# First stage of a vision layer: GpSimd subtracts the low parts of Q's weights from pieces that ScalarE scales in place, and K's and V's low parts are made four tokens later

## What is computed

```python
# token stage: one S4 convolution kernel per batch row b (64), token h (128), 1024 positions l
dt = exp(log_dt); dt_Lambda = dt * Lambda          # complex, 128 tokens x 64 states
Wc = W * (exp(dt_Lambda) - 1) / (exp(dt_Lambda * 1024) - 1) / Lambda
K  = real(einsum('chn,hnl->chl', Wc, exp(dt_Lambda * pos)))      # W is the input x; h = K, (64, 128, 1024)
# layer stage, per batch row of 128 tokens
h = h + attention(layernorm(h), Wq, Wk, Wv, Wo)    # 32 heads of 32, 8 kv heads, rotary, causal
h = h + ffn(layernorm(h), A, B, Wr, br)            # 8 low-rank experts, softmax router
```

## Time and profile before

| | before |
|---|---|
| median of 3 runs | 2348.03 us (2345.55 to 2348.85) |
| profiled execution, its own time | 2350.26 us |
| its span | 2348.1 us |
| TensorE busy / VectorE / ScalarE / GpSimd over the span | 95% / 77% / 75% / 75% |
| VectorE busy in each stretch of 10 us from 40 to 230 us | 8.9 to 10.0 us |
| last matmul of the first stage ends | 239.3 us |
| first instruction of the second block | 244.6 us |

### The profile page before, as it was taken

The page is one execution under the profiler, slowest core; times in us unless marked ns, Lnnn a source line. Parts: engine busy times, 40 slices in busy tenths (PEclk is TensorE's granted clock), DMA queues, the critical chain, the costliest instruction groups (busy, mean ns, idle before and its releaser), DMA issues.

```text
span 2348.1 us, 49641 instructions
## 1 busy us (share of the span) xinstructions
PE 2231.6 (95%) x14040; PEld 1147.6 (49%) x14040; DVE 1818.7 (77%) x7750; ACT 1760.8 (75%) x6141; POOL 1750.0 (75%) x1550
## 2 busy tenths in 40 slices
PE   3898699999999999999999999999999999999986
PEld 2777344444444444444444444444444444444442
DVE  8999467777777777777777777877777777777864
ACT  5787477777787777777777777777778777778772
POOL 3776387777777778777778778788777777778772
PEclk9999899999999999999999999999999999999988
DMA  3888599999999999999999999999999999999994
GB/s 95 268 268 259 126 176 181 193 188 186 194 194 186 189 196 181 195 193 186 192 194 188 187 191 192 188 195 191 186 197 190 189 192 192 181 196 192 190 166 105
DMA packets 1205661, 443.10 MB, mean 189 GB/s; under 512 B 1155718, under 2 KB 1158022, under 8 KB 1205388
## 3 DMA queue, kind: packets, MB, share of 16 engines
q1 hardware_dynamic: 1205380, 439.93, 95.9%
q10 hardware_dynamic: 8, 0.01, 0.0%
HBM read 87.43 MB, written 67.11 MB: 66 GB/s over the span
## 4 chain that ended last, share of the span: by engine, by line
PE 67%; DMA 6%; POOL 6%; DVE 4%; SPq 3%; issue 2%; ACT 2%; POOLq 0%; DVEq 0%; ACTq 0%
PE pc L910 11%; PE pb L910 10%; PE pa L910 10%; DMA pt<-p 4%; PE pb L896 4%; PE pb L898 4%; PE pb L897 4%; PE pa L896 4%; PE pa L897 4%; PE pa L898 4%; PE pv_ps L939 3%; PE s_ps L924 3%; POOL p L1436 3%; POOL pr L1428 2%; DMA h_ln<-h 2%
## 5 line engine op out<-in xcount | busy, mean ns | idle before, releaser
L1063 ACT ACTIVATE pr<-pr,smin 128x64 f32<-128x64 f32 (+1 forms) x2048 | 738.8, 362 | 185.3 <-DVE smin L1207 184.4
L1428 POOL TENSOR_TENSOR pr<-pr,rinv 128x512 f32<-128x512 f32 x512 | 577.0, 1137 | 367.8 <-DVE rinv L1215 366.8
L1436 POOL TENSOR_TENSOR p<-pr,p 128x512 f16<-128x512 f32 x512 | 590.9, 1158 | 66.6 <-ACT p L1073 64.6
L1207 DVE CUSTOM_DVE_ANT_0 pr<-s_ps,cst 128x64 f32<-128x64 f32 (+1 forms) x2048 | 404.2, 252 | 219.0 <-PE s_ps L924 119.0
L1073 ACT ACTIVATE p<-pr 128x512 f16<-128x512 f32 x512 | 320.1, 625 | 257.8 <-DMA pt<-p 133.6
L1063 ACT ACTIVATION_READ_ACCUMULATOR pr<-pr,smin 128x1 f32 x2048 | 382.3, 187 | 0.0
L910 PE MATMUL pa<-wkv_hi,xt 128*128 128x512 f16 x1024 | 326.5, 380 | 13.4 <-DMA xt<-xs 13.4
L910 PE MATMUL pb<-wq_hi,xt 128*128 128x512 f16 x1024 | 326.9, 381 | 0.0
L910 PE MATMUL pc<-wq_hi,xt 128*128 128x512 f16 x1024 | 315.2, 379 | 0.0
L635 PE MATMUL hps<-z,xw 128*128 128x256 f32 x792 | 178.8, 386 | 60.5 <-POOL xw L363 38.2
L896 PE MATMUL pa<-wo_hi,ctx_t 128*128 128x512 f16 x512 | 195.5, 382 | 2.0 <-DVE ctx_t L1221 1.8
(11 more groups left out here) (185 smaller groups left out, 4723.5 us busy)
## 6 DMA issues: line engine op xcount, KB each, us to landing
h<-rows SPq DMA_DIRECT2D x128, 256.0 KB, 4.0
h_res<-h SPq DMA_DIRECT2D x64, 512.0 KB, 4.6
out<-rows SPq DMA_DIRECT2D x64, 512.0 KB, 3.4
h_ln<-h SPq DMA_DIRECT2D x63, 512.0 KB, 4.5
pt<-p SPq DMA_TRANSPOSE x512, 4.1
xa<-x SPq DMA_DIRECT2D x16, 256.0 KB, 4.4
xb<-x SPq DMA_DIRECT2D x32, 128.0 KB, 3.8
wst<-wq SPq DMA_DIRECT2D x8, 512.0 KB, 4.9
```

The costliest lines, as they stand in the source:

```text
L1063: last = A.activation(p, p, ACT.Exp, bias=smin[g % 2][:, j:j + 1], scale=-1.0, accum_out=rsum[g % 2][:, j:j + 1])
L1207: V.tensor_tensor_reduce(pr[g % 2][:, cols], s_ps[g % 2][:, cols], masks[h], 1.0, 3e38, ALU.add, ALU.min, smin[g % 2][:, j:j + 1]).then_in ...
L1428: nc.gpsimd.tensor_tensor(p3, p3, rinv[g % 2][:, :].unsqueeze(2).broadcast_to([P, HG, P]), ALU.mult).then_inc(p_norm, 1)
L1436: nc.gpsimd.tensor_tensor(p[:, HG * P:], pr[g % 2][:, :], p[:, 0:HG * P], ALU.subtract).then_inc(pl_done, 1)
```

## The change

- Q's low parts are no longer made by VectorE. ScalarE, right behind each Q piece's high part, multiplies the piece in its buffer by 64 in place (one more instruction for each of 8 pieces), and GpSimd subtracts the high part from it, at the end of window 3 of the chunk (behind `add`).
- K's and V's low part stays on VectorE and moves from the end of window 0 to the end of window 1 of the next chunk. O's stays at the end of window 3, those of `aw` and `bm` at the ends of windows 5 and 9. In the last chunk O's and K's and V's come at the very end, as before.
- SyncE waits for GpSimd's count where the buffer held a Q piece, for VectorE's elsewhere, and its waits and loads move with the low parts: from the third chunk on, Q's next piece from window 1 to window 2 of the chunk, ahead of O's, and K's and V's from window 3 to window 0 of the next.

```diff
-LOW_LATER = 1
+        def low_at(piece):
+            at, name, k, _, _ = piece
+            return WINDOWS if k == CHUNKS - 1 and name != "wq" else at + (2 if name in ("wq", "wkv") else 1)
+
+        def pieces_before(n, on_pool):
+            return sum((name == "wq") == on_pool for _, name, _, _, _ in PIECES[:n])
...
-                    if n >= WR:
-                        sp.wait_ge(w_lo, n - WR + 1)
+                    if n >= WR and PIECES[n - WR][1] == "wq":
+                        sp.wait_ge(wq_low, pieces_before(n - WR + 1, True))
+                    elif n >= WR:
+                        sp.wait_ge(w_lo, pieces_before(n - WR + 1, False))
...
-                    while loaded < len(PIECES) and PIECES[loaded - WR][0] + LOW_LATER <= w + 1:
+                    while loaded < len(PIECES) and low_at(PIECES[loaded - WR]) <= w + 1:
                         load_weight(loaded)
...
+                def wq_lo(n):
+                    _, name, k, width, _ = PIECES[n]
+                    pool.wait_ge(wq_scaled, k + 1)
+                    nc.gpsimd.tensor_tensor(weight("wq_lo", k), wst[n % WR][:, 0:width], weight("wq_hi", k),
+                                            ALU.subtract).then_inc(wq_low, 1)
...
                     add(w)
+                    for n, piece in enumerate(PIECES):
+                        if piece[1] == "wq" and low_at(piece) == w:
+                            wq_lo(n)
...
-                    A.activation(weight(name + "_hi", k), wst[n % WR][:, 0:width], ACT.Copy, scale=WS).then_inc(w_hi, 1)
+                    staged = wst[n % WR][:, 0:width]
+                    A.activation(weight(name + "_hi", k), staged, ACT.Copy, scale=WS).then_inc(w_hi, 1)
+                    if name == "wq":
+                        A.activation(staged, staged, ACT.Copy, scale=WS).then_inc(wq_scaled, 1)
...
                     for n, piece in enumerate(PIECES):
-                        if piece[0] + LOW_LATER == w:
+                        if low_at(piece) == w and piece[1] != "wq":
                             weight_lo(n)
-                weight_lo(len(PIECES) - 1)
+                for n, piece in enumerate(PIECES):
+                    if low_at(piece) == WINDOWS and piece[1] != "wq":
+                        weight_lo(n)
```

More of the change, by code:

```diff
@@ L219, in s4_stage @@
         w_lo = sem("w_lo")
+        wq_scaled = sem("wq_scaled")
+        wq_low = sem("wq_low")
         tab_v = sem("tab_v")
```

## The result

The changed kernel takes 2362.28 us (median of 5 runs, 2360.26 to 2363.53) against 2348.03 us: 1.0056 times the time before, 95% interval 1.0044 to 1.0067 (the bare quotient of the two medians is 1.0061). The profiled execution took 2363.53 us, its span is 2361.7. In a second measurement, on another chip, the same kernel took 2360.35 against 2350.14 us there, 1.0044 times (1.0027 to 1.0060). The forecast was 2358.5 us and slower.

A forecast was written before the change was run, and what follows sets the result against it. VectorE was taken to set the pace (busy 24.81 of 24.91 us), a closed loop after the change. Terms +2.6, -0.8, +1.1, +6.4 and +1.2 gave +10.5 us: median 2348.0 to 2358.5, likeliest range 2354 to 2364, wide 2340 to 2366.

The forecast's parts named there:

- up to the first `wo_lo`: Start to VectorE's first `wo_lo`: later `table_i` and GpSimd's chain give 63.2 us against 60.61, +2.6.
- first cycle: First stretch from one VectorE `wo_lo` to the next: 26.4 us against 27.19, as `aw_lo`'s wait falls away, -0.8.
- the four others: Last four of six cycles, `wo_lo` to `wo_lo`: 26.3 to 26.9 us against 24.9, together +6.4.
- end of the stage: Window 30: `sum_z` meets the last `add`, then the subtraction, +2.3 us, less the removed `wq_lo`, 1.13: +1.2.
- VectorE and GpSimd take turns: Their instructions with two SBUF inputs never run together; `wkv_lo` loses its 2.2 us wait, `tables` waits, `digits` follows the `add`.
- The subtraction: GpSimd, behind window 3's `add`: 1024 columns, 2.25 us, bounds 2.1 and 2.6, added to the chain.
- ScalarE's 0.95 us: Scaling pass over 1024 columns behind `wq_hi`, ahead of the sines: `theta` comes 0.95 us later.
- The closed loop: TensorE's windows 3 and 0, ScalarE, GpSimd's chain, `tables`: `table_i` at 14.3 plus chain 12.0, cycle at least 26.3 us.
- SyncE's moved loads I cost at nothing: First-stage load queue: stores behind moved loads late by under 1 us; otherwise up to +1.3 a cycle, +8 in all.
- Rival 1: First stage: the subtraction does not keep VectorE from its turns; cycles 23.3 us, -14, total 2334; chance 0.11.
- Rival 2: `digits` gets its turn between `digits_m2` and the `add`, 2.36 off the chain; cycles 24.0 us, -7, 2341; chance 0.12.
- Rival 3: Half the waits, `theta` about 1 us earlier than said; cycles 25.2 us, total 2348 to 2352; chance 0.15.

The follow-up runs named there:

- e11: Changed kernel with GpSimd's subtraction over 64 of the 1024 columns of each Q piece: 2353.60 us, 1.0021 times the kernel before.
- e3: Changed kernel without ScalarE's scaling, so GpSimd subtracts from the unscaled Q piece: 2353.61 us, 1.0031 times the kernel before.
- e7: Changed kernel with SyncE's load into the buffer of O's piece issued one window later: 2359.45 us, 1.0041 times the kernel before.
- e10: Changed kernel with GpSimd's `add` for window 0 held back until VectorE's `digits` are done: 2364.66 us, 1.0062 times the kernel before.
- e4: Changed kernel with ScalarE's three sines moved to the end of window 0, ahead of Q's high part: 2348.91 us, 1.0014 times the kernel before.
- e6: Kernel before with ScalarE's three sines moved to the end of window 0, ahead of Q's high part: 2352.02 us, 1.0009 times the kernel before.
- e2: Changed kernel with K's and V's low parts back at the end of window 0; Q's stays on GpSimd: 2362.50 us, 1.0063 times the kernel before.
- e1: Kernel before with only K's and V's low parts made four tokens later; Q's stays on VectorE: 2344.17 us, 0.9989 times the kernel before.

## Why the prediction was right, point by point

**Direction and size.** Slower, with the reason named. The first stage was forecast 10.5 us longer and is 8.5 to 8.9; the other 5.1 us of the first measured difference (14.25 us) lie in the second block, of which the prediction said nothing. Without these 5.1 us the median would have been near 2357, below the forecast and not above it (an estimate, 2348.0 + 8.9). In the second pair of profiles the marks are 10.5 apart. Term by term, from the first pair:

| term | forecast | measured |
|---|---|---|
| up to the first `wo_lo` | +2.6 | +1.8 |
| first cycle | -0.8 | -0.2 |
| second cycle | +1.1 | +0.4 |
| the four others | +6.4 | +6.1 |
| end of the stage | +1.2 | +0.8 |

**VectorE and GpSimd take turns: right.** It carries all the rest. `wkv_lo` at 0.68 us, `tables` at 2.84 and L504 behind the `add`, at 2.57, are as foretold. But the 2.84 of `tables` came by another order, so that this number is in part luck: I had `tables` wait for the subtraction in all cycles. That is so in the first two (2.61 us, from 81.81 on, the chain from `table_i` to `wo_lo` 11.67). In the others `table_i` ended after `sum_z` was issued, `sum_z` went ahead of the `add`, and `tables` waited for the `add` (185.13 to 187.93) and ran ahead of the subtraction. The chain is then 11.43 instead of 12.0. In the first two cycles L504 is issued late in the `add` and lasts only 0.82 us. The reading of `digits` in the sum of VectorE's own work was off, too: they hold it for 0.87 us (162.76 to 163.63 in the earlier trace rows), not 0.67; the chain does not use that figure.

**The subtraction: right, and a little cheaper than taken.** It took 2.13 us where it ran unhindered (55.44); 2.25 was taken, with bounds of 2.1 and 2.6. e11 shows its worth: 7.8 us of the first stage.

**ScalarE's 0.95 us: right.** The start-to-start is 0.94, and e3 takes 0.7 to 0.9 us off each of the last three cycles.

**The closed loop: right in kind, wrong in one link.** I closed it through TensorE's 12.3 us of windows 3 and 0 without a gap, so that window 0 is done at 10.5, with TensorE idle for some 3 us ahead of window 3. The third cycle has such a gap (2.20 us, from 111.58 to 113.78). In the fifth TensorE's timeline is another:

```profile
159.77 12.67 PE L659 MATMUL hps<-z,xw 128*128 128x256 f32 x56 [1.99 <-ACT rows L433]
173.37 10.60 PE L659 MATMUL hps<-z,xw 128*128 128x256 f32 x48 [0.94 <-issue]
```

The first row is windows 2 and 3, the second windows 0 and 1. TensorE waits for ScalarE's evicts ahead of window 2, and starts window 0 at 173.37, 4.2 us after `wo_lo`, right behind VectorE's first `table_z` for it; with 5.42 us for its 24 matmuls it is done at 9.6. What holds `theta` back there is a store (3.02 and 0.61 us above): `wq_hi` starts at 11.45 and `table_i` at 14.7, 0.4 later than the 14.3 taken. In the second, fourth and sixth cycle these two starts are the same within 0.1 us. In the second ScalarE waits 0.92 us for a store; in the fourth and sixth the profile puts the 3.13 and 2.01 us ahead of the same evict down to TensorE, but in e7, with the load out of the way, that evict runs at 6.2 instead of 8.0 to 8.2.

The term that was too small is thus "SyncE's moved loads I cost at nothing", with its buffers late "by under 1 us": one was 3 us late. The fallback beside it was up to 1.3 us a cycle, and e7 shows 1.3 us of `theta` and 1.1 of a cycle for that queue. The store behind O's load is issued 1.6 us after `wo_lo` in both kernels (140.34 before, 170.81 after). Before the change the evict of window 0's first token ran 5.5 us behind it (145.82) and waited last for TensorE; now it runs 6.2 us behind it (177.04) and waits for the store. The store lands at least 0.7 us later, and TensorE's earlier window 0 no longer covers it. New just ahead of that store is the moved load of Q's piece (167.13). That this load delays it is read from the rows; no run moves it alone. The chain of 11.4 instead of 12.0 and the 0.4 of `theta` nearly cancel, so the close agreement of the cycles (26.1 to 26.2, where 26.3 was the least) is in part luck.

The other late cycles have TensorE at half clock: `table_i` at 15.77 in the third, with 80 matmuls in 19.19 us, and at 15.31 in the first, where a wait of 1.08 us for a store adds to it. The prediction had no fall of the clock in the first stage; before, show 1.00 throughout.

**The rivals.** Rival 1, the subtraction hides, is refuted by e11. Rival 2 is refuted in both its parts: `digits` did not get the turn, and e10, where they do, is no faster. Rival 3, about as before, would have needed `theta` 1 us earlier, which it was not; e4, where it is 0.8 to 1.6 us earlier in the last three cycles, has 1.0014, so its arithmetic held. The loss is thus this small sum of places: 2.1 us of subtraction, 0.95 of scaling and a store, all put on a path that had slack before (e6), while what was taken away, 3.3 us of VectorE, was on it.

The sentence of the Trainium skill (page Perfetto Trace Analysis, section Optimizing Scalar/DVE Operations), that moving an operation between VectorE and GpSimd might not help as they share a read port, held: e2, the move alone, loses 0.63% (1.0063). The rows show that the two take turns; the loss beyond "might not help" comes from where the turns lie on the chain.

## What to carry to other kernels

When two engines take turns, an instruction moved from the one to the other still takes the turn for its whole length: look not at either engine's idle time but for what is issued behind it, and at which link of the chain that sets the cycle it lands. Draw that chain through all engines, the DMA queue's in-order waits too; here a load that waits for a low part held up a store, an evict and the sines. And try the order before the placement: with K's and V's part made later, three sines put ahead of one pass and one load put behind the stores gave 0.4% (0.9957), of which the first step alone is 0.1% (e1), where the change with its moved subtraction lost 0.6% (1.0056).

## What was not expected of the hardware

- TensorE's granted clock stood at 0.50 (1.2 GHz) for stretches of 3.4 us in the middle of the first stage. In e2's cycles and the changed kernel's they began within 1.4 us of the end of an idle time of 1.9 to 3.0 us; 80 matmuls took 19.2 instead of 17.5 us. After other idle times of 2.20 us (e7, 189.78) and 1.99 us (the changed kernel, 159.77) it stayed at full. In the kernel before, with at most 1.7 us between its matmuls from the first cycle to the last and 2.29 us once behind them, it did not fall in the first stage.
- A GpSimd subtraction of 1024 columns, f32 and f16 in and f16 out, takes 2.13 us, where the addition in f32 takes 2.36.
- The same instructions in the second block took 2092.1 to 2100.5 us in 14 profiles, without a cause that these runs show.
